# Attention with 32 heads: a small subtraction moves from GpSimd to VectorE, and the sign of its row is turned

## The chip, the cores and the metric

The kernel runs on one core of a Trainium2 chip. The metric is device time in microseconds (us) of one execution. Before the change three runs took 4368.01, 4374.25 and 4378.47 us; their median is 4374.25 us. Engines are named as the profile names them: PE is TensorE (matmul), PEld its weight load, DVE is VectorE, ACT is ScalarE, POOL is GpSimd, SP is SyncE, which here only issues DMAs.

## The reference, cut to what matters

The whole program is eight layers of a network on x of shape (8, 512, 128). The change lies in one of them, an attention with 32 heads of width 32 in each of 8 batch items (worked on in groups of 4 heads: 8 groups in an item, 64 in all):

```python
scale = DIM_HEAD ** (-0.5)
qkv = (x @ w_qkv).reshape(b, n, 3, HEADS, DIM_HEAD)
q, k, v = ...                                  # (b, heads, n, 32)
dots = jnp.einsum('bhnd,bhmd->bhnm', q, k) * scale
attn = jax.nn.softmax(dots, axis=-1)           # exp(dots - max) / sum
out = jnp.einsum('bhnm,bhmd->bhnd', attn, v)
```

## The kernel before, in words

`attend_wide` is the function. It computes the scores twice. The first time (`scores`, L837) queries are rows, and DVE takes each row's maximum from PSUM (`tensor_reduce`, L1046, into `top`). The second time (`shifted_scores`, L843) keys are rows, and the maximum of each query is subtracted inside the matmul: two more rows of the operands carry it, in `q4` the maximum itself and in `k4` a constant, -1.0, set by POOL at L721. ACT then takes the exponential straight from PSUM (L966, into `e`). For precision each number is split in a high part, rounded to fp32r, and a low part, the difference; so there are two rows, one for the high and one for the low part of the maxima.

The way of the maxima, for one group: ACT rounds all 16 columns of `top` into `tops[:, 0]` (`high_tops`, L954); POOL subtracts that from `top` into `tops[:, 1]` (`low_tops`, L726); DVE turns the 128x32 tile (`turn_tops`, L1030, into `topsT`); SP sends it with four small DMAs into the two rows of `q4` (L775); PE needs the rows at the start of the next step.

The work is a pipeline over groups, written out by hand. A step treats group n at stage 0 (projections of q and k; high part by ACT at L939, low part by DVE at L1022; three DMAs of 256 KB for q at L768 and three for k at L781, all on SP's one queue), the group before it at stage 1 (scores and maxima), the one before at stage 2 (the way of the maxima), at stage 3 (shifted scores and exponentials) and at stages 4 and 5 (product with v, sums, normalising). Each engine walks through sixteen places (j, b) of a step, j the head and b the block, and the code says at which place a small operation is put: on DVE the maximum of a place comes first, then what is put there. `low` for q stands at (0, 1), `turn_tops` at (0, 3), `low` for k at (1, 1). On PE `project_k` stands at (0, 3) and `project_v` at (1, 3); `project_v` waits for the low part of k, since they share a PSUM bank. PE starts a step when the six loads of q and k of the group have landed (`loaded`, 16 each) and, for stage 3, when the four row DMAs have (`row_loaded`).

POOL adds pairs of exponential blocks (`e_pair`, L741, four instructions of 128x1024 in a step, with both inputs in SBUF) and multiplies once (`o_norm`, L749). The first of the four waits for PE's sums of the group before (L865, at PE's place (3, 0)). POOL does `low_tops` between the second and the third pair.

Of the kernel before, what the change touches and what calls it, by code (L numbers as in the profile page):

```python
# [20 lines left out]
ALU = mybir.AluOpType  # L21
ACT = mybir.ActivationFunctionType
F32 = mybir.dt.float32
# [9 lines left out]
KROWS = 96  # L33
# [36 lines left out]
def wait(eng, sem, value):  # L70

    if isinstance(value, int) and value <= 0:
        return
    eng.wait_ge(sem, value)
# [572 lines left out]
def attend_wide(nc, g, name, scale):  # L647
# [10 lines left out]
    with Phase(nc, name) as ph:  # L658
# [6 lines left out]
        k4 = [ph.sb(f"k4_{r}", [P, HG, S], F32R) for r in range(RQ)]  # L665
        v4 = [ph.sb(f"v4_{r}", [P, TB, P]) for r in range(2)]
        top = ph.sb("top", [P, 2, HG, TB])
        tops = ph.sb("tops", [P, 2, HG, TB], F32R)
# [11 lines left out]
        set_up, w_loaded = ph.sem("set_up"), ph.sem("w_loaded")  # L680
# [6 lines left out]
        s_ready, max_done, hi_done, lo_done, tops_turned, st_ready, exp_done, pair_done, pv_done, o_copied = (  # L687
            ph.sem(k) for k in ("s_ready", "max_done", "hi_done", "lo_done", "tops_turned", "st_ready", "exp_done",
                                "pair_done", "pv_done", "o_copied"))
# [14 lines left out]
        def next_batch(st):  # L704

            return st.c == U and not (isinstance(st.i, int) and st.i + 1 >= B)

        def run(eng, step):

            for i in range(B):  # L710
                for c in range(1, U + 1):
                    step(Step(i, c, NG, U))
            for c in range(1, 6):
                step(Step(B, c, NG, U))

        with nc.Block() as block:
            @block.gpsimd
            def _(pool):

                for r in range(RQ):  # L720
                    pool.memset(k4[r][KROWS:KROWS + 2].bitcast(F32), -1.0).then_inc(set_up, 1)  # L721

                def low_tops(st):
                    n, t = st.n(2), st.slot(2, 2)
                    pool.wait_ge(hi_done, n)
                    pool.tensor_tensor(tops[:, 1], top[:, t], tops[:, 0].bitcast(F32), ALU.subtract).then_inc(lo_done, 1)  # L726

                def step(st):
                    if st.has(2) and not st.has(4):
                        low_tops(st)  # L730
                    if st.has(4):
                        n, r = st.n(4), st.slot(4, 2)
                        for j in range(HG):
                            if j == 2 and st.has(2):
                                low_tops(st)

                            pool.wait_ge(exp_done, 16 * (n - 1) + 4 * j + 4)
                            if j == 0:

                                wait(pool, sums_done, n - 1)  # L740
                            pool.tensor_tensor(e_pair[:, j, :, :], e[r][:, j, 0:2, :], e[r][:, j, 2:4, :], ALU.add  # L741
                                               ).then_inc(pair_done, 1)
                    if st.has(5):
                        n = st.n(5)
                        pool.wait_ge(o_copied, n)
                        pool.wait_ge(r_done, n)

                        wait(pool, y_ready, n - 1)
                        pool.tensor_tensor(o_norm[:], o_sb[st.slot(5, 2)][:], r_sb[:], ALU.mult).then_inc(o_done, 1)  # L749

                run(pool, step)
# [162 lines left out]
            @block.scalar  # L914
            def _(act):
                def copy_out(st):
                    n = st.n(4)
                    act.wait_ge(pv_done, n)

                    wait(act, o_done, n - 2)  # L920
                    act.activation(o_sb[st.slot(4, 2)][:], g.ps[:, PV_BANK, :], ACT.Copy).then_inc(o_copied, 1)

                def copy_x(batch):
                    act.wait_ge(xp_ready, batch)
                    act.activation(xT[:], g.ps[:, PROJ_BANK, :], ACT.Copy).then_inc(xT_done, 1)

                def copy_x_for_v(st):
                    act.wait_ge(xT_done, st.i + 1)

                    wait(act, v_ready, st.n(4))  # L930
                    act.activation(xT_v[:], xT[:], ACT.Copy).then_inc(xT_v_done, 1)

                def high(st, bank, ready, hi, factor, done):

                    act.wait_ge(ready, st.n(0))
                    if st.has(1):

                        act.wait_ge(loaded[st.slot(1, RQ)], 16 * 6 * st.use(1, RQ))
                    act.activation(hi[:], g.ps[:, bank, :], ACT.Copy, scale=factor).then_inc(done, 1)  # L939

                def copy_v(st):
                    n, r = st.n(3), st.slot(3, 2)
                    act.wait_ge(v_ready, n)

                    wait(act, pv_done, n - 2)
                    act.activation(v4[r][:], g.ps[:, PROJ_BANK, :].rearrange("p (t c) -> p t c", t=TB), ACT.Copy
                                   ).then_inc(v_done, 1)

                def high_tops(st):
                    n, t = st.n(2), st.slot(2, 2)  # L950
                    act.wait_ge(max_done, 16 * n)

                    wait(act, tops_turned, n - 1)
                    act.activation(tops[:, 0], top[:, t], ACT.Copy).then_inc(hi_done, 1)  # L954

                def step(st):
                    for j in range(HG):
                        for b in range(TB):
                            if st.has(3):
                                n, r = st.n(3), st.slot(3, 2)  # L960
                                act.wait_ge(st_ready, 16 * (n - 1) + 4 * j + b + 1)
                                if j == 0 and b == 0:

                                    wait(act, pv_done, n - 2)
                                    wait(act, sums_done, n - 2)
                                act.activation(e[r][:, j, b, :], g.ps[:, ST_BANK + b % 2, :], ACT.Exp  # L966
                                               ).then_inc(exp_done, 1)
                            if (j, b) == (0, 0) and st.has(0):
                                high(st, PROJ_BANK, q_ready, q_hi, scale, q_hi_done)
                            if (j, b) == (0, 1) and st.has(2):  # L970
                                high_tops(st)
                            if (j, b) == (1, 0) and st.has(0):
                                high(st, PROJ_BANK, k_ready, k_hi, 1.0, k_hi_done)
                            if (j, b) == (1, 1) and st.has(3) and st.c == 4:
                                copy_x_for_v(st)
                            if (j, b) == (2, 0) and st.has(3):
                                copy_v(st)
                            if (j, b) == (1, 3) and st.has(4):
                                copy_out(st)
                            if (j, b) == (3, 2) and next_batch(st):  # L980

                                act.wait_ge(k_ready, st.n(0))
                                act.wait_ge(xT_v_done, st.i + 1)
                                copy_x(st.i + 2)

                copy_x(1)
                run(act, step)

            @block.vector
            def _(dve):  # L990
# [7 lines left out]
                def recip(st):  # L998
                    n = st.n(5)
                    dve.wait_ge(l_turned, n)  # L1000
                    dve.reciprocal(r_tok[:], r_sb[:].rearrange("p (c b) -> p c b", b=32)[:, :, 0]
                                   ).then_inc(recip_done, 1)
# [14 lines left out]
                def low(st, bank, hi_done, hi, lo, factor, done):  # L1017

                    dve.wait_ge(hi_done, st.n(0))
                    if st.has(1):  # L1020
                        dve.wait_ge(loaded[st.slot(1, RQ)], 16 * 6 * st.use(1, RQ))
                    dve.scalar_tensor_tensor(lo[:], g.ps[:, bank, :], factor, hi[:].bitcast(F32), ALU.mult,  # L1022
                                             ALU.subtract).then_inc(done, 1)

                def turn_tops(st):
                    n = st.n(2)
                    dve.wait_ge(lo_done, n)
                    if st.has(3):
                        dve.wait_ge(row_loaded[st.slot(3, RQ)], 16 * 4 * st.use(3, RQ))
                    dve.transpose(topsT[:].bitcast(F32), tops[:].rearrange("p h j t -> p (h j t)").bitcast(F32)  # L1030
                                  ).then_inc(tops_turned, 1)
# [4 lines left out]
                def step(st):  # L1036
                    for j in range(HG):
                        for qb in range(TB):
                            if st.has(1):
                                n, t = st.n(1), st.slot(1, 2)  # L1040
# [8 lines left out]
                                low(st, PROJ_BANK, q_hi_done, q_hi, q_lo, scale, q_lo_done)  # L1049
                            if (j, qb) == (0, 1) and st.has(5):  # L1050
                                recip(st)
                            if (j, qb) == (0, 3) and st.has(2):
                                turn_tops(st)
                            if (j, qb) == (1, 0) and st.has(5):
# [1621 lines left out]
```

## Time and profile before

| | |
|---|---|
| runs | 4368.01, 4374.25, 4378.47 us |
| the profiled execution | 4368.01 us, its span 4366.3 us |
| PE busy | 3458.4 us (79%) |
| DVE busy | 3185.1 us (73%) |
| ACT busy | 2437.9 us (56%) |
| POOL busy | 1204.1 us (28%) |
| TensorE's granted clock, mean | 0.902 |
| this attention | about 1290 to 2530 us of the span |

The span is the time from the first to the last instruction of the program; the device time adds 1.7 us. A row of the timeline gives the start, the duration, the engine, the line of the source, what is written and read, and how many instructions of a kind stand in it; in brackets the idle time before it and what ended that. In a row of x2 the duration runs from the start of the first to the end of the second. A weight load or a matmul that waited for a DMA names it.

### The profile page before, as it was taken

How to read it: one execution, taken by the hardware profiler on the slowest of the kernel's cores; microseconds unless marked ns; L12 is line 12 of the kernel's file. 1: busy time of each engine (PE TensorE's matmuls, PEld its weight loads, DVE VectorE, ACT ScalarE, POOL GpSimd, SP SyncE). 2: the span in 40 equal slices, each digit the busy share in tenths (PEclk: the TensorE clock that was granted, in tenths of full speed). 3: DMA queues.
4: the chain of work that ended last, by engine and by line, in shares of the span. 5: the costliest groups of instructions: out<-in, count | busy, mean ns of one | idle time of the engine just before them, and what ended most of it. 6: DMA issues, size and time to landing. Idle time of an engine off the chain costs nothing. (4 is left out here: it accounts for less than half of the span.)

```text
span 4366.3 us, 58109 instructions
## 1 busy us (share of the span) xinstructions
PE 3458.4 (79%) x18272; PEld 2101.5 (48%) x18272; DVE 3185.1 (73%) x7262; ACT 2437.9 (56%) x4422; POOL 1204.1 (28%) x798
## 2 busy tenths in 40 slices
PE   5788888677938999999999937892599998657736
PEld 2555555456714555554555425671366665422214
DVE  3999999566845767767777556684488885789986
ACT  2788888445714656555556514571399997312103
POOL 0000000043413555555555615341000000044520
PEclk9899999888968999999999968896799999877767
DMA  5333332113346766666666401331643432000000
GB/s 183 57 63 64 65 49 34 30 49 122 137 92 79 91 88 90 88 86 88 88 88 88 62 30 50 121 136 55 190 62 43 63 60 41 6 20 5 5 28 25
DMA packets 287698, 307.97 MB, mean 71 GB/s; under 512 B 98031, under 2 KB 187567, under 8 KB 287268
## 3 DMA queue, kind: packets, MB, share of 16 engines
q1 hardware_dynamic: 277668, 283.27, 36.8%
q0 software_dynamic: 9728, 20.99, 1.4%
q8 instruction: 151, 2.47, 0.3%
q14 instruction: 151, 1.24, 0.1%
HBM read 124.40 MB, written 78.05 MB: 46 GB/s over the span
## 5 line engine op out<-in xcount | busy, mean ns | idle before, releaser
L1046 DVE TENSOR_REDUCE at_b_top<-ps 128x1 f32<-128x512 f32 x1024 | 660.9, 682 | 376.5 <-PE ps L837 375.6
L966 ACT ACTIVATE at_b_e<-ps 128x512 f32<-128x512 f32 x1024 | 583.4, 598 | 475.3 <-PE ps L843 461.8
L550 ACT ACTIVATE at_a_e<-at_a_logits,at_a_neg_top 128x512 f32<-128x512 f32 x1024 | 656.2, 716 | 157.0 <-DVE at_a_neg_top L610 155.5
L741 POOL TENSOR_TENSOR at_b_e_pair<-at_b_e 128x1024 f32<-128x1024 f32 x256 | 603.4, 2377 | 479.4 <-PE ps L865 476.9
L474 PE MATMUL ps<-at_a_k,at_a_q 96*128 96x512 f32 x1024 | 477.3, 491 | 185.2 <-DVE at_a_clipped L578 117.3
L837 PE MATMUL ps<-at_b_k,at_b_q 96*128 96x512 f32 x1024 | 501.3, 493 | 40.4 <-DMA at_b_k<-at_b_k_hi 38.1
L543 ACT ACTIVATE at_a_eT<-ps 128x512 f32<-128x512 f32 x896 | 461.3, 588 | 0.7 <-PE ps L487 0.2
L843 PE MATMUL ps<-at_b_q,at_b_k 98*128 98x512 f32 x1024 | 427.5, 419 | 19.1 <-ACT at_b_e L966 18.7
L606 DVE CUSTOM_DVE_ANT_0 at_a_logits<-ps,at_a_strip 128x512 f32<-128x512 f32 x512 | 340.4, 689 | 109.5 <-issue 32.4
L578 DVE TENSOR_SCALAR at_a_clipped<-ps 128x512 f32<-128x512 f32 x512 | 352.0, 688 | 39.8 <-PE ps L474 38.7
L474 PEld LDWEIGHTS ps<-at_a_k,at_a_q 96*128 96x128 f32 x1024 | 185.1, 190 | 397.2 <-DVE at_a_clipped L578 206.4
L600 DVE CUSTOM_DVE_ANT_0 at_a_logits<-at_a_clipped,at_a_decay_strip 128x512 f32<-128x512 f32 x512 | 346.9, 682 | 0.0
L837 PEld LDWEIGHTS ps<-at_b_k,at_b_q 96*128 96x128 f32 x1024 | 197.4, 193 | 274.9 <-issue 110.6
L487 PE MATMUL ps<-ident,at_a_e 128*128 128x128 f32 x2048 | 291.7, 276 | 2.3 <-ACT at_a_eT L543 2.3
L487 PE MATMUL ps<-flip,at_a_e 128*128 128x128 f32 x2048 | 287.8, 273 | 0.2
L1343 POOL TENSOR_TENSOR lin_z<-lin_z,lin_zmax 64x1024 f32<-64x1024 f32 x8 | 31.4, 3926 | 878.1 <-DVE lin_zmax L1440 878.1
L2298 ACT ACTIVATE moe_gate<-ps 128x512 f32<-128x512 f32 x240 | 143.7, 599 | 226.6 <-PE ps L2202 164.4
L487 PEld LDWEIGHTS ps<-ident,at_a_e 128*128 128x128 f32 x2048 | 251.9, 142 | 35.1 <-ACT at_a_e L550 2.5
L843 PEld LDWEIGHTS ps<-at_b_q,at_b_k 98*128 98x128 f32 x1024 | 194.1, 190 | 152.3 <-ACT at_b_e L966 131.0
L487 PEld LDWEIGHTS ps<-flip,at_a_e 128*128 128x128 f32 x2048 | 248.6, 141 | 32.6 <-issue 1.2
L2423 DVE TENSOR_TENSOR moe_h<-moe_gate,ps 128x512 f32<-128x512 f32 x240 | 164.9, 687 | 129.5 <-ACT moe_gate L2298 108.5
L2150 POOL DMA_INDIRECT y_slots<-moe_y_tok,moe_idx x176 | 176.6, 1003 | 282.9 <-DVE moe_y_tok L2411 242.0
(332 smaller groups left out, 6463.3 us busy)
## 6 DMA issues: line engine op xcount, KB each, us to landing
moe_stage<-in_moe_w SPq DMA_DIRECT2D x46, 768.0 KB
at_b_q<-at_b_q_hi SPq DMA_DIRECT2D x128, 256.0 KB, 5.1
at_b_k<-at_b_k_hi SPq DMA_DIRECT2D x128, 256.0 KB, 7.9
v<-in_a_va SPq DMA_DIRECT2D x64, 256.0 KB, 3.7
at_a_v<-v SPq DMA_DIRECT2D x64, 256.0 KB, 7.2
at_b_q<-at_b_q_lo SPq DMA_DIRECT2D x64, 256.0 KB, 7.6
at_b_k<-at_b_k_lo SPq DMA_DIRECT2D x64, 256.0 KB, 8.0
slot_rows<-empty_slots SPq DMA_DIRECT2D x44, 288.0 KB, 6.7
```

The costliest lines, as they stand in the source:

```text
L474: pe.matmul(g.ps[:, S_BANK + qb % 2, :], q4[r][0:KROWS, j, qb * P:(qb + 1) * P], k4[r][0:KROWS, j, :], start=True, stop=True).then_inc(s_r ...
L487: ins = pe.transpose(bank, block, g.ident[:] if decay else g.flip[:])
L543: act.activation(eT[r][:, j, kb, :], g.ps[:, TR_BANK + kb, :], ACT.Copy).then_inc(tr_read[kb], 1)
L550: act.activation(e[:, j, qb, :], logits[:, j % 2, qb, :], ACT.Exp, bias=neg_top[:, j % 2, qb:qb + 1]).then_inc(exp_done, 1)
L578: dve.tensor_scalar(clipped[:, qb, :], g.ps[:, S_BANK + qb % 2, :], -CLAMP, CLAMP, ALU.max, ALU.min).then_inc(clip_done, 1)
L600: dve.tensor_tensor_reduce(logits[:, j % 2, qb, :], clipped[:, qb, :], decay_strip[:, cols], 1.0, -3e38, ALU.mult, ALU.max, top[:, j % 2, ...
L606: dve.tensor_tensor_reduce(logits[:, j % 2, qb, :], g.ps[:, S_BANK + qb % 2, :], strip[:, j, cols], 1.0, -3e38, ALU.add, ALU.max, top[:, j ...
L741: pool.tensor_tensor(e_pair[:, j, :, :], e[r][:, j, 0:2, :], e[r][:, j, 2:4, :], ALU.add).then_inc(pair_done, 1)
L837: pe.matmul(g.ps[:, bank, :], q4[r][0:KROWS, j, qb * P:(qb + 1) * P], k4[r][0:KROWS, j, :], start=True, stop=True).then_inc(s_ready, 1)
L843: pe.matmul(g.ps[:, ST_BANK + kb % 2, :], k4[r][0:KROWS + 2, j, kb * P:(kb + 1) * P], q4[r][0:KROWS + 2, j, :], start=True, stop=True).the ...
L966: act.activation(e[r][:, j, b, :], g.ps[:, ST_BANK + b % 2, :], ACT.Exp).then_inc(exp_done, 1)
L1046: dve.tensor_reduce(top[:, t, j, qb:qb + 1], g.ps[:, bank, :], AX_X, ALU.max).then_inc(max_done, 1)
```

## The change

The subtraction `low_tops` leaves POOL. DVE does it as one `scalar_tensor_tensor`, at place (0, 2), behind the third maximum of the step and ahead of the fourth. ACT now rounds the negated maxima (`scale=-1.0`), DVE computes -top minus the rounded part, and the constant in `k4` becomes +1.0, so the product in the matmul is the same number. The instruction that waits for `hi_done` is now on DVE.

```diff
-                    pool.memset(k4[r][KROWS:KROWS + 2].bitcast(F32), -1.0).then_inc(set_up, 1)
-
-                def low_tops(st):
-                    n, t = st.n(2), st.slot(2, 2)
-                    pool.wait_ge(hi_done, n)
-                    pool.tensor_tensor(tops[:, 1], top[:, t], tops[:, 0].bitcast(F32), ALU.subtract).then_inc(lo_done, 1)
+                    pool.memset(k4[r][KROWS:KROWS + 2].bitcast(F32), 1.0).then_inc(set_up, 1)
 
                 def step(st):
-                    if st.has(2) and not st.has(4):
-                        low_tops(st)
                     if st.has(4):
                         n, r = st.n(4), st.slot(4, 2)
                         for j in range(HG):
-                            if j == 2 and st.has(2):
-                                low_tops(st)
...
-                    act.activation(tops[:, 0], top[:, t], ACT.Copy).then_inc(hi_done, 1)
+                    act.activation(tops[:, 0], top[:, t], ACT.Copy, scale=-1.0).then_inc(hi_done, 1)
...
+                def low_tops(st):
+                    n, t = st.n(2), st.slot(2, 2)
+                    dve.wait_ge(hi_done, n)
+                    dve.scalar_tensor_tensor(tops[:, 1], top[:, t], -1.0, tops[:, 0].bitcast(F32), ALU.mult,
+                                             ALU.subtract).then_inc(lo_done, 1)
...
+                            if (j, qb) == (0, 2) and st.has(2):
+                                low_tops(st)
                             if (j, qb) == (0, 3) and st.has(2):
                                 turn_tops(st)
```

On DVE, in a step of the middle of this attention, this stood before, from the low part of q (L1022) over the second pair of maxima to the low part of k:

```order
L1022 SCALAR_TENSOR_TENSOR at_b_q_lo<-ps,at_b_q_hi 128x512 [waits at_b0_loaded0,at_b0_q_hi_done]
L1001 RECIPROCAL at_b_r_tok<-at_b_r_sb 128x16 [waits at_b0_l_turned]
L1046 TENSOR_REDUCE at_b_top<-ps 128x1 [waits at_b0_s_ready] x2
L1030 STREAM_TRANSPOSE at_b_topsT<-at_b_tops 128x32 [waits at_b0_row_loaded2,at_b0_lo_done]
L1046 TENSOR_REDUCE at_b_top<-ps 128x1 [waits at_b0_s_ready]
L1007 STREAM_TRANSPOSE at_b_r_sb<-at_b_r_tok 128x512 [waits at_b0_recip_done]
```

And this stands there now (the line numbers of the changed file differ by a few):

```order
L1013 SCALAR_TENSOR_TENSOR at_b_q_lo<-ps,at_b_q_hi 128x512 [waits at_b0_loaded0,at_b0_q_hi_done]
L992 RECIPROCAL at_b_r_tok<-at_b_r_sb 128x16 [waits at_b0_l_turned]
L1043 TENSOR_REDUCE at_b_top<-ps 128x1 [waits at_b0_s_ready]
L1019 SCALAR_TENSOR_TENSOR at_b_tops<-at_b_top,at_b_tops 128x16 [waits at_b0_hi_done]
L1043 TENSOR_REDUCE at_b_top<-ps 128x1 [waits at_b0_s_ready]
L1027 STREAM_TRANSPOSE at_b_topsT<-at_b_tops 128x32 [waits at_b0_row_loaded2,at_b0_lo_done]
L1043 TENSOR_REDUCE at_b_top<-ps 128x1 [waits at_b0_s_ready]
L998 STREAM_TRANSPOSE at_b_r_sb<-at_b_r_tok 128x512 [waits at_b0_recip_done]
```

One instruction with the wait for ACT's rounding has come in between two maxima; everything else on DVE keeps its place. On POOL this stood before, for one step:

```order
L741 TENSOR_TENSOR at_b_e_pair<-at_b_e 128x1024 [waits at_b0_sums_done,at_b0_exp_done]
L741 TENSOR_TENSOR at_b_e_pair<-at_b_e 128x1024 [waits at_b0_exp_done]
L726 TENSOR_TENSOR at_b_tops<-at_b_top,at_b_tops 128x16 [waits at_b0_hi_done]
L741 TENSOR_TENSOR at_b_e_pair<-at_b_e 128x1024 [waits at_b0_exp_done] x2
L749 TENSOR_TENSOR at_b_o_norm<-at_b_o_sb,at_b_r_sb 128x512 [waits at_b0_y_ready,at_b0_r_done,at_b0_o_copied]
```

And now, for one step:

```order
L732 TENSOR_TENSOR at_b_e_pair<-at_b_e 128x1024 [waits at_b0_sums_done,at_b0_exp_done]
L732 TENSOR_TENSOR at_b_e_pair<-at_b_e 128x1024 [waits at_b0_exp_done] x3
L740 TENSOR_TENSOR at_b_o_norm<-at_b_o_sb,at_b_r_sb 128x512 [waits at_b0_y_ready,at_b0_r_done,at_b0_o_copied]
```

The four pairs now follow one another with nothing between them that waits for ACT's rounding.

## Rows read from the trace of the kernel before

**Rows 1.** Busy time of each engine over this attention, granted clock, DMA share, GB/s.

```profile
core 0: us, PE busy (x) PEld busy (x) DVE busy (x) ACT busy (x) POOL busy (x), PEclk, DMA share, GB/s
1290.00:2530.00 1240.00, 1180.20 (x6392) 606.52 (x6392) 833.27 (x1438) 708.46 (x1358) 691.13 (x383) 0.98 0.65 84
```

**Rows 2.** Waits of the weight loads, 1400 to 2480 us: total, times, longest.

```profile
PEld ps L837 <- DMA at_b_k<-at_b_k_hi: 25.9, 57, 1.0
```

**Rows 3.** Timeline of PE at two starts of a step (third row: the later start).

```profile
1898.46 0.50 PE L837 MATMUL ps<-at_b_k,at_b_q 96*128 96x512 f32 x1 [0.17 <-DMA at_b_k<-at_b_k_hi]
...
1916.38 0.50 PE L843 MATMUL ps<-at_b_q,at_b_k 98*128 98x512 f32 x1
1916.77 0.50 PE L837 MATMUL ps<-at_b_k,at_b_q 96*128 96x512 f32 x1
```

**Rows 4.** Timeline of SP's queue in the step from 1898.46 to 1916.77.

```profile
1901.64 1.20 SPq L768 DMA_DIRECT2D at_b_q<-at_b_q_hi  x2
...
1904.27 2.64 SPq L775 DMA_DIRECT2D at_b_q<-at_b_topsT  x4
1907.15 0.59 SPq L781 DMA_DIRECT2D at_b_k<-at_b_k_hi  x1
```

**Rows 5.** The DMA engines within that step, columns as in the first group.

```profile
1902.50:1914.50 12.00, 11.76 (x72) 6.65 (x71) 8.36 (x14) 7.50 (x14) 5.00 (x3) 1.00 1.02 130
```

**Rows 6.** Timelines of SP and PE in the fourth and the sixth step.

```profile
1340.88 1.19 SPq L768 DMA_DIRECT2D at_b_q<-at_b_q_hi  x2
...
1345.47 0.59 SPq L781 DMA_DIRECT2D at_b_k<-at_b_k_hi  x1
...
1356.29 0.79 PE L837 MATMUL ps<-at_b_k,at_b_q 96*128 96x512 f32 x1 [5.44 <-DMA at_b_k<-at_b_k_hi]
...
1380.73 1.19 SPq L768 DMA_DIRECT2D at_b_q<-at_b_q_hi  x2
...
1386.76 0.59 SPq L781 DMA_DIRECT2D at_b_k<-at_b_k_hi  x1
...
1396.33 0.39 PE L837 MATMUL ps<-at_b_k,at_b_q 96*128 96x512 f32 x1
```

**Rows 7.** Timeline of DVE around the change, step from 1898.46.

```profile
1902.83 1.29 DVE L1046 TENSOR_REDUCE at_b_top<-ps 128x1 f32<-128x512 f32 x2 [1.06 <-PE ps L837]
1904.04 0.20 DVE L1030 STREAM_TRANSPOSE at_b_topsT<-at_b_tops 128x32 f32<-128x32 f32 x1
1904.64 0.69 DVE L1046 TENSOR_REDUCE at_b_top<-ps 128x1 f32<-128x512 f32 x1 [0.40 <-PE ps L837]
...
1906.45 0.67 DVE L1022 SCALAR_TENSOR_TENSOR at_b_k_lo<-ps,at_b_k_hi 128x512 fp32r<-128x512 f32 x1
```

**Rows 8.** Timeline of POOL in the same step.

```profile
1896.62 4.71 POOL L741 TENSOR_TENSOR at_b_e_pair<-at_b_e 128x1024 f32<-128x1024 f32 x2 [7.72 <-PE ps L865]
1901.35 0.22 POOL L726 TENSOR_TENSOR at_b_tops<-at_b_top,at_b_tops 128x16 fp32r<-128x16 f32 x1
1901.53 4.73 POOL L741 TENSOR_TENSOR at_b_e_pair<-at_b_e 128x1024 f32<-128x1024 f32 x2
```

**Rows 9.** A small instruction of the same kind on DVE: busy us, mean ns.

```profile
L138 DVE SCALAR_TENSOR_TENSOR st_ffn_t<-st_ffn_t,st_ffn_var 128x32 f32<-128x32 f32 x6 | 1.2, 192 | 0.2
```

**Rows 10.** Linear attention: timelines of POOL and DVE, then one line's ns min/median/max.

```profile
3936.52 2.33 POOL L1343 TENSOR_TENSOR lin_z<-lin_z,lin_zmax 64x1024 f32<-64x1024 f32 x1 [22.13 <-DVE lin_zmax L1440]
...
3937.68 1.73 DVE L1450 TENSOR_TENSOR lin_yT<-lin_y 128x512 f32<-128x512 f32 x1
...
L1450 DVE TENSOR_TENSOR lin_yT<-lin_y x8: 693/1734/1735, 3892.3 to 4202.4; 128x512 f32<-128x512 f32 x8
```

**Rows 11.** Linear attention: POOL's products beside DVE's scans, ns min/median/max.

```profile
L1361 POOL TENSOR_TENSOR lin_prod<-lin_state,lin_phi x56: 1254/2172/2181, 3866.2 to 4185.9; 128x512 f32<-128x512 f32 x56
```

**Rows 12.** Timelines of POOL and DVE in the step after the longest one.

```profile
1840.00 4.70 POOL L741 TENSOR_TENSOR at_b_e_pair<-at_b_e 128x1024 f32<-128x1024 f32 x2 [7.54 <-PE ps L865]
...
1846.74 1.29 DVE L1046 TENSOR_REDUCE at_b_top<-ps 128x1 f32<-128x512 f32 x2 [1.08 <-PE ps L837]
```

**Rows 13.** Timeline of PE: the projection of v, step from 1898.46.

```profile
1908.13 1.06 PE L829 MATMUL ps<-at_b_w,at_b_xT_v 128*128 128x128 f32 x8
```

## The prediction, made before the changed kernel ran

> **What bounds the kernel now.** I read the busy time by stretch first. The change lies in the 1240 us from 1290 to 2530, with 64 groups, so about as many steps. PE is busy 1180 of them, DVE 833, POOL 691 [rows 1]. That looks like a stage bound by PE, and the second view corrects it. Of the 59 steps between 1400 and 2480 us, 57 begin with a weight load that waited for the last load of k [rows 2]. The timeline of PE shows it in place: the first matmul at 1898.46 waited for that DMA, and at the next start, 1916.77, 0.39 us lie between two matmuls that otherwise stand closer [rows 3]. So a step ends when the third load of k lands, and its length is a loop: PE projects q, ACT and DVE split it, SP issues q's loads 3.18 us after the start (1901.64), then the rows of maxima (1904.27), then k's loads (1907.15) [rows 4]; the DMA engines are full without a gap from 1902.5 to 1914.5 [rows 5], and k lands just ahead of 1916.77. From 1396.33 to 1898.46 there are 27 steps [rows 3, 6]: 502.13 / 27 = 18.60 us each. PE alone needs less: the step from 1898.46 took 18.31, with 0.15 or so of waiting in it, so 18.15 to 18.3.
>
> What matters is then not how busy DVE or POOL is, but whether the change makes (a) q's loads start later, (b) k's loads land later, or (c) PE itself take over 18.6 us in a step.
>
> **What it removes.** POOL loses 64 subtractions of 0.22 us (14 us). POOL waited 7.72 us in the step for PE's sums [rows 8] and has that slack every step, so this is worth nothing. Its effect is on phase: the third and fourth pair now start 0.22 us earlier or more. The turn on DVE did not wait for POOL: the subtraction ended at 1901.57, the turn began at 1904.04 behind the fourth maximum [rows 7, 8]. So no wait is removed either. The factor -1.0 on ACT and the +1.0 in two rows are the same instructions with other constants: 0.
>
> **What it adds.** 64 small instructions on DVE. The nearest row is the same operation on 32 columns, 192 ns [rows 9]; following instructions start about 80 ns before the one ahead ends, so 0.11 us each in a row. It waits for ACT's rounding, which had ended by 1901.35, when POOL began to use it [rows 8], while DVE gets there at 1903.44 (the fourth maximum's start: 1902.83 plus the 0.61 by which two maxima are apart) [rows 7]. So the added wait is over 2 us early. Queued behind it are the fourth maximum, the turn, the fifth maximum and k's low part. DVE idles 0.40 us ahead of the fifth [rows 7], so the plain cost, 0.11 and at most 0.22 us, ends there. Only the rows' DMAs go out 0.1 to 0.2 us later, and k's loads behind them at most as much.
>
> Does a later issue of k's loads matter? In the fourth step they went out 4.59 us after q's, and the next step began 15.41 us after q's (1340.88, 1345.47, 1356.29). In the sixth they went out 6.03 us after, and the next began 15.60 after [rows 6]. The step at 1898.46 has 5.51 and 15.13 [rows 3, 4]. Issue 1.44 us later, landing at most 0.19 us later: the loads queue behind q's in full DMA engines anyway. So up to half a microsecond there costs nothing. By this sum alone the change is worth 0.
>
> **The term that can cost.** The added instruction reads `top` and `tops[:, 0]`, both in SBUF, while POOL runs its pairs, which read SBUF too. Nothing on DVE in this stage did so. In the linear attention something does: `lin_yT<-lin_y`, two inputs in SBUF, took 1.73 us in seven of its eight executions and 0.693 in the one without POOL. In the shown case it began at 3937.68, POOL's instruction ended at 3938.85, it ended at 3939.41: 0.56 after POOL's end, though it needs 0.69 [rows 10]. So it stood still until 0.14 us before POOL's recorded end and then ran. The products of POOL beside DVE's scans go from 1254 to 2172 ns in the same manner, by turns, one instruction of each [rows 11].
>
> The Trainium skill has this as a rule (SBUF — State Buffer, "Who interferes with whom"): a VectorE instruction with two SBUF inputs and a GpSimd instruction that reads SBUF exclude each other for the whole instruction, and the one that comes second fully blocks. By that rule, the trace agrees, at 1.73 against 0.69 us.
>
> So what counts is where DVE's 1903.44 falls among POOL's pairs. POOL's pairs start 2.33 us apart. Without the subtraction the fourth starts 7.0 us after the first: 1896.62 + 7.0 = 1903.62 [rows 8]. DVE asks at 1903.44, 0.18 us before the third pair gives way. It waits 0.1 to 0.2 us, harmless by the slack above. But had it asked just after 1903.62, it would wait for the fourth pair: 2.38 - 0.14 = 2.24 us. I worked this distance out in the same way for 59 steps (from the first pair's start and the fourth maximum's; first 0.59 us, last 0.15): mean 0.2, on time in 53, late in 6, and under 0.1 us on time in 7 more. The late ones follow the longest steps: after the one of 19.1 us the fourth pair starts at 1840.00 + 7.0 = 1847.00 and DVE asks at 1846.74 + 0.61 = 1847.35 [rows 12].
>
> Price of a late step: the fourth maximum starts 2.24 + 0.11 later, at 1905.79; the turn 1906.40; the fifth 1906.52 instead of 1904.64, so 1.88 later, and so is the end of k's low part (1907.12, now 1909.00) [rows 7]. PE's projection of v, at 1908.13, waits for that low part [rows 13]: PE stands 0.9 us. PE's step becomes 18.15 + 0.9 to 18.3 + 0.9, against 18.60: 0.45 to 0.6 us more. k's loads go out behind the rows at 1906.6 + 2.64 = 1909.25, 7.6 us after q's; the trace shows up to 6.03 hidden. Beyond that, between 0 and 1.6 us. I take 0.5 for a late step, since the DMA engines still have q's data then, and keep 0.45 to 1.6. A late step also protects the next: it has no wait for landing, and that wait is what makes DVE late against POOL.
>
> **Sum.** 6 late steps, 8 with a few of the near ones, times 0.5 = 4 us; the rest 0. The profiled execution took 4368.01, so 4372. That execution lies 6.2 below the median of the runs, 4374.25; by the median the forecast is 4378. About 0.2% (9 us) is what a measurement of this kernel can tell from no change.
>
> **Rivals.**
> - The edge lies elsewhere (slower). The start and the lock need not coincide to 0.1 us. If the decision falls 0.15 to 0.2 us against DVE, over half the steps are late; since a late step makes the next on time, some 24 of 59 are. At 0.5 to 0.8 us that is 12 to 19 us: 4390. For it: the mean distance is as small as the uncertainty. Against: in the linear attention both engines' turns are clean.
> - POOL, with its next pair queued, gets in ahead of DVE each time. Then DVE waits out the fourth pair in all 59 steps, with 0.2 to 0.5 us on top: k's low part 2.3 us late, PE stands 1.3 to 1.45, the step 19.5 to 19.6, 1.0 more: +59, 4433. Against: the alternation [rows 11].
> - The small instruction is not held up, because it is so short. Then nothing is left of the cost: 4374.
> - Faster: taking POOL out of the chain from maxima to rows lets something start earlier. The only place is the start and end of the stage, where a few waits of under 2 us could go; 4372. Over 9 us would need the DMA loop to shorten by 0.15 us in each step, and its start (q's low part) is ahead of the change.
>
> **Chances.** Forecast 0.56; edge elsewhere 0.24; POOL ahead each time 0.06; not held up 0.10; faster path 0.04. Slower by over 0.2%: most of the second case, the third, and a small part of the first, 0.30. Faster by over 0.2%: 0.05, with the scatter of the loop. Within: 0.65. The range 4367 to 4395 takes in the scatter of the runs before below, and 24 late steps at 0.8 us above; it leaves out the third case and a late step of 1.6 us.
>
> **What would show it.** DVE's new instruction takes from 0.2 to 0.7 us where POOL's third pair is about to end, and 2.3 to 2.5 us in a late step; a count of the two gives the number. In late steps PE's projection of v waits for k's low part. Elsewhere steps still start on k's landing, 18.6 us apart, with k's loads issued up to 0.4 us later. If the instruction always takes 0.2 us, the lock is not there for it; if it takes over 2 us in most steps, the forecast is wrong; and if k lands later in steps where it took 0.5, the claim that the issue is hidden is wrong.

## The result, and the profile after

The changed kernel takes 4400.49 us (median of five runs, 4398.01 to 4405.13), the kernel before 4371.31 (five runs, 4367.10 to 4378.47). The ratio is 1.0056, 95% interval 1.0041 to 1.0070: slower by 0.41 to 0.70%. On record beside it are 22 runs of the changed kernel, the five among them (4382.46 to 4406.04, median 4397.12); it fits these, while the two medians above alone would give 1.0067. The forecast was 4378 with a range to 4395. In the profiled executions the span went from 4366.3 to 4388.6 us, 22.3 us more, and all of it lies in this attention, which now ends about 23 us later:

```profile
core 0: us, PE busy (x) PEld busy (x) DVE busy (x) ACT busy (x) POOL busy (x), PEclk, DMA share, GB/s
1290.00:2553.00 1263.00, 1184.01 (x6392) 604.15 (x6392) 907.45 (x1502) 707.27 (x1358) 679.33 (x319) 0.98 0.62 82
```

Against [rows 1] PE's busy time is the same within 4 us, the granted clock too. DVE shows 74 us more for 64 added instructions, over 1 us each, where a like one took 0.19 [rows 9]: they stand and wait. The distribution for that one line, in ns min/median/max:

```profile
L1019 DVE SCALAR_TENSOR_TENSOR at_b_tops<-at_b_top,at_b_tops x64: 165/660/3633, 1321.9 to 2515.2; 128x16 fp32r<-128x16 f32 x64
```

Now the waits, 1400 to 2500 us (total us, times, longest). The first row is of PE and new; the second, of the weight loads, answers to [rows 2], where the number was 57 (in a window 20 us shorter):

```profile
PE ps L820 <- DVE at_b_k_lo L1013: 20.5, 24, 1.1
...
PEld ps L828 <- DMA at_b_k<-at_b_k_hi: 15.7, 36, 1.0
```

In 24 steps PE's projection of v stood for k's low part. I took the 58 steps from the sixth on one by one (start of the first matmul to the next start). In 25 the added instruction takes over 2 us; I call these late. They last 19.48 us on average, the other 33 last 18.54. Before the change the same 58 steps last 18.57 on average (the 18.60 of the prediction is from 27 of them). So the late ones add 25 x 0.91 = 22.7 us and the others save 1.1: together 21.6 of the 22.3 us.

One such step, and the step after it, in the timelines of POOL and DVE:

```profile
1791.28 9.41 POOL L732 TENSOR_TENSOR at_b_e_pair<-at_b_e 128x1024 f32<-128x1024 f32 x4 [7.03 <-PE ps L856]
...
1811.07 9.39 POOL L732 TENSOR_TENSOR at_b_e_pair<-at_b_e 128x1024 f32<-128x1024 f32 x4 [7.03 <-PE ps L856]
```

```profile
1797.69 3.04 DVE L1019 SCALAR_TENSOR_TENSOR at_b_tops<-at_b_top,at_b_tops 128x16 fp32r<-128x16 f32 x1
1800.65 0.68 DVE L1043 TENSOR_REDUCE at_b_top<-ps 128x1 f32<-128x512 f32 x1
...
1803.15 0.67 DVE L1013 SCALAR_TENSOR_TENSOR at_b_k_lo<-ps,at_b_k_hi 128x512 fp32r<-128x512 f32 x1
...
1817.50 0.66 DVE L1019 SCALAR_TENSOR_TENSOR at_b_tops<-at_b_top,at_b_tops 128x16 fp32r<-128x16 f32 x1
```

The pairs are 2.34 us apart, so the fourth starts at 1798.30 and at 1818.09. DVE asks (the recorded start of its instruction) at 1797.69 and at 1817.50: 0.61 and 0.59 us ahead of the fourth pair. The second time it gets in when the third pair ends. The first time it is there just as early and POOL's fourth pair goes first; DVE ends at 1800.73, with the fourth pair (1791.28 + 9.41 = 1800.69). PE, at the projection of v, and the two starts around the step:

```profile
1792.80 0.39 PE L828 MATMUL ps<-at_b_k,at_b_q 96*128 96x512 f32 x1
...
1803.91 1.13 PE L820 MATMUL ps<-at_b_w,at_b_xT_v 128*128 128x128 f32 x8 [1.09 <-issue]
...
1812.58 0.41 PE L828 MATMUL ps<-at_b_k,at_b_q 96*128 96x512 f32 x1
```

PE stands 1.09 us ahead of the projection, which begins as k's low part ends (1803.15 + 0.67); the trace names no releaser in this one case of the 25. The step takes 19.78 us; the next, by its start at 1830.80, 18.22. Of the 25 late instructions, 4 asked after the fourth pair had begun, 12 asked 0.06 to 0.18 us ahead of it, and 9 asked 0.31 to 0.61 us ahead and still lost. Of the 33 others, 6 asked 0.11 to 0.20 us ahead and 27 over 0.3 us ahead.

### The profile page after: what moved, and what is told of

Read it like the earlier page. It is cut to its first block and busy times, and to the rows that moved or that the text cites. A ratio compares the mean times of both kernels' runs of the same rounds, so it can differ in the third digit from the quotient of the medians.

```text
span 4388.6 us, 58109 instructions
## 1 busy us (share of the span) xinstructions
PE 3462.0 (79%) x18272; PEld 2099.5 (48%) x18272; DVE 3259.7 (74%) x7326; ACT 2437.3 (56%) x4422; POOL 1191.8 (27%) x734
```

## The experiments

Theory: a VectorE instruction with two inputs in SBUF and a GpSimd instruction that reads SBUF exclude each other, and the late steps are all of the cost. Each kernel has 4 to 11 runs, compared with 12 or 21 of the kernel before on the same chip: medians 4367.8 us for e1 to e4, 4369.2 for e5 to e8, 4367.1 for e9 to e11. Steps are counted in the one profiled execution of each.

**e1, the move alone.** The signs as before.

```diff
-  dve.scalar_tensor_tensor(tops[:, 1], top[:, t], -1.0, tops[:, 0].bitcast(F32), ALU.mult, ALU.subtract)
+  dve.tensor_tensor(tops[:, 1], top[:, t], tops[:, 0].bitcast(F32), ALU.subtract)
-  act.activation(tops[:, 0], top[:, t], ACT.Copy, scale=-1.0)          # and the rows 1.0
+  act.activation(tops[:, 0], top[:, t], ACT.Copy)                      # and the rows -1.0
```

> The subtraction moved to VectorE alone, as a tensor_tensor, with the signs as before the change (factor 1 on ScalarE, -1.0 in the two rows). Theory (VectorE and GpSimd exclude each other while both read SBUF): as the changed kernel, 20 to 30 of 58 steps with the small instruction over 2 us long, 20 to 35 us slower than before. Rival (the sign, another operation, or the scale on ScalarE costs): within 5 us of before.

Measured: 4394.80 us, ratio 1.0059 (1.0046 to 1.0073), 29 late steps (a thirtieth instruction took 1.99 us). The sign, the scale and the kind of instruction show no effect; the move is all.

**e2, POOL out of the way; e10, only ahead of the fourth pair.**

```diff
   for j in range(HG):
+      if j == 2 and st.has(2):          # e10: j == 3
+          pool.wait_ge(lo_done, st.n(2))
       pool.wait_ge(exp_done, ...)
```

> The changed kernel, but GpSimd waits for the small instruction of VectorE before its third pair, so that it is idle when VectorE asks. Theory (exclusion): the small instruction takes 0.2 us in all 64 cases, no late step, the time of before within 5 us; GpSimd's third and fourth pair end 2 us later, at about 9.9 us of the step, which nobody awaits before 14.6. Rival (the instruction and its wait in VectorE's row cost by themselves): stays 20 to 35 us slower than before. Rival (GpSimd's pairs are near the path): slower than the changed kernel.

> The changed kernel, but GpSimd waits for VectorE's small instruction before its fourth pair (not its third). VectorE still meets the third pair and waits up to its end. Theory (what costs is only the fourth pair getting in ahead): the small instruction takes 0.2 to 0.7 us, never over 1; no late step; within 5 us of before. Rival (meeting a pair at all costs): 10 us or more slower than before.

Measured: e2 4369.26 us, 1.0001 (0.9992 to 1.0010); e10 4370.19 us, 1.0007 (0.9997 to 1.0016). No late step in either. The same instruction with the same wait at the same place of DVE, in e2:

```profile
L1021 DVE SCALAR_TENSOR_TENSOR at_b_tops<-at_b_top,at_b_tops x64: 162/166/1116, 1325.5 to 2494.9; 128x16 fp32r<-128x16 f32 x64
```

So the instruction in DVE's row costs nothing; neither does meeting the third pair, in e10 (median 242 ns, against 166 here). The one of 1.1 us here and those of 1.3 and 1.1 in e10 lie behind the 58 steps. Only the fourth pair costs.

**e3, one operand in SBUF.** The low part of the maxima is left out: its row stays zero.

```diff
-  dve.scalar_tensor_tensor(tops[:, 1], top[:, t], -1.0, tops[:, 0].bitcast(F32), ALU.mult, ALU.subtract)
+  dve.tensor_reduce(scr[:], <tops[:, 0] as 128x16x1>, AX_X, ALU.max)
```

> The changed kernel with a small instruction of VectorE at the same place, behind the same wait, that reads one 128x16 operand from SBUF instead of two and writes a spare tile; the low part of the maxima is left out (its row stays zero). Theory (two inputs in SBUF are what excludes): the small instruction takes about 0.17 us always, no late step, the time of before within 5 us. Rival (any instruction there costs, or any reading beside GpSimd): 20 to 35 us slower than before, small instruction still up to 2.7 us.

Measured: 4367.30 us, 0.9995 (0.9986 to 1.0004).

```profile
L1020 DVE TENSOR_REDUCE at_b_scr<-at_b_tops x64: 157/159/170, 1324.9 to 2494.5; 128x16 f32<-128x16 f32 x64
```

At most 170 ns in 64 cases, beside the same pairs. This changed the kind of instruction along with the number of inputs. That the kind is not the reason can be read in the changed kernel: q's low part is the same operation as the added one, runs beside the pairs too (POOL's second), and has one input in PSUM and one in SBUF. It was never held up:

```profile
L1013 DVE SCALAR_TENSOR_TENSOR at_b_q_lo<-ps,at_b_q_hi x64: 674/681/692, 1282.7 to 2478.9; 128x512 fp32r<-128x512 f32 x64
```

So a second input in SBUF is what makes it wait.

**e4, asking earlier.** The instruction at (0, 1), where DVE idles 1.1 us afterwards.

```diff
-  if (j, qb) == (0, 2) and st.has(2):
+  if (j, qb) == (0, 1) and st.has(2):
       low_tops(st)
```

> The changed kernel with the small instruction at place (0, 1), behind the reciprocal. VectorE asks about 3.2 us after the step's start, at or just after the start of GpSimd's third pair (2.8 to 3.2), so it waits 1.9 to 2.4 us nearly always, 1.1 of which it idled before. If it gets in at every pair's end: k's low part 0.5 us later, ahead of the projection of v, no late step, within 5 us of before although the instruction takes 2 us. If GpSimd's queued next pair gets in ahead in a share of the cases (9 of some 40 in the changed kernel): that share has a wait of 4.3 us and a step of over 20 us; 12 such steps make 20 us or more over before.

Measured: 4419.45 us, 1.0114 (1.0099 to 1.0130). In 14 of the 58 steps DVE asked at the very end of the second pair, by the records 0.01 us ahead of the third, and always got in, in 0.11 us. In the other 44 it met the third. In 25 of these it got in at that pair's end, after 1.6 to 2.3 us, and the steps last 18.61 us on average, as the same 25 did before (18.60): 2 us of wait, nothing lost. But 19 of the 44 times POOL's fourth pair went ahead and DVE stood over 4 us:

```profile
1762.30 9.37 POOL L732 TENSOR_TENSOR at_b_e_pair<-at_b_e 128x1024 f32<-128x1024 f32 x4 [7.43 <-PE ps L856]
```

```profile
1767.23 4.48 DVE L1019 SCALAR_TENSOR_TENSOR at_b_tops<-at_b_top,at_b_tops 128x16 fp32r<-128x16 f32 x1
```

DVE was there 2.1 us ahead of the fourth pair (1762.30 + 7.02) and ended at 1771.71 with it. Coming early doesn't help.

The 19 steps fall in two groups. Eight last 20.35 us on average. The other eleven last 22.10, this one among them, since TensorE's granted clock fell in them as well. PE had waited for a maximum behind DVE's long instruction; then the clock was 0.50, the lower of its two levels (1.2 of 2.4 GHz):

```profile
1772.37 0.50 PE L828 MATMUL ps<-at_b_k,at_b_q 96*128 96x512 f32 x1 [1.99 <-DVE at_b_top L1043]
```

```profile
1774.00:1776.00 2.00, 2.00 (x12) 0.21 (x4) 1.39 (x3) 0.00 (x0) 1.27 (x1) 0.50 0.04 6
```

The sixteen products with v behind that wait took 3.25 us instead of 1.92. In the other eight the clock stayed at 1.00, though PE had waited 1.5 to 2.1 us in them and 1.7 to 2.1 in the eleven; what decides is open. In the kernel before and in the changed one the clock fell in none of the 58 steps, so it has no part in the 22 us.

**e5, the reading alone.** The kernel before, with a spare instruction.

```diff
+  if (j, qb) == (0, 2) and st.has(2):
+      dve.wait_ge(hi_done, st.n(2))
+      dve.scalar_tensor_tensor(scr[:], top[:, st.slot(2, 2)], -1.0, tops[:, 0].bitcast(F32), ALU.mult, ALU.subtract)
```

> The kernel before, GpSimd keeping its subtraction, with one more instruction on VectorE at place (0, 2): the same two inputs in SBUF, written to a spare tile nobody reads. Theory (exclusion): GpSimd's fourth pair starts about 0.22 us later here than in the changed kernel, so VectorE always asks ahead of it; no step is late by missing the edge, and late steps come only where GpSimd's queued fourth pair gets in ahead of the waiting VectorE, 20 to 45% of the steps as in the runs so far: 12 to 26 late steps of about 0.9 us, 10 to 24 us slower than before. If only the missed edge counted: within 5 us of before.

Measured: 4388.77 us, 1.0041 (1.0029 to 1.0054). All 58 asked 0.41 to 0.79 us ahead of the fourth pair; 12 lost to it, with steps of 19.94 us on average. The missed edge is thus not needed for a loss.

**e6, one wait in every step.** The instruction at (0, 3).

```diff
-  if (j, qb) == (0, 2) and st.has(2):
+  if (j, qb) == (0, 3) and st.has(2):
       low_tops(st)
```

> The changed kernel with the small instruction at place (0, 3), behind the fourth maximum. VectorE asks at 5.6 us of the step, after GpSimd's fourth pair has begun (5.1 to 5.5) and waits to that pair's end (7.4 to 7.8) in nearly every step; behind that pair stands o_norm, which waits for VectorE, so nothing gets in ahead. Theory: 50 or more of 58 instructions take 1.7 to 2.2 us, k's low part ends at about 10.3 us, the projection of v 0.6 us late, each step 0.3 to 0.5 longer, evenly: 17 to 29 us slower than before. Rival (a late step costs by the irregularity, not by PE's wait): under 10 us.

Measured: 4413.29 us, 1.0101 (1.0086 to 1.0115): 44 us where 17 to 29 were expected. The instruction waits for the end of the fourth pair in all 58 steps, as expected; a step takes 19.30 us. PE's projection of v starts at 10.35 to 10.64 us of the step (mean 10.53), against 9.68: 0.85 late where I had expected 0.6. Behind it 8.7 to 8.9 us follow, against 8.89 on average before, so little of the delay is made good. I had taken PE's own step for 18.15 to 18.3; by 9.68 + 8.70 it is nearer 18.35.

**e7, shorter pieces.** Each pair cut in two.

```diff
-  pool.tensor_tensor(e_pair[:, j, :, :], e[r][:, j, 0:2, :], e[r][:, j, 2:4, :], ALU.add).then_inc(pair_done, 1)
+  for h in range(2):
+      ins = pool.tensor_tensor(e_pair[:, j, h, :], e[r][:, j, h, :], e[r][:, j, 2 + h, :], ALU.add)
+  ins.then_inc(pair_done, 1)
```

> The changed kernel with each of GpSimd's four pairs cut in two instructions of 128x512 (eight of about 1.2 us instead of four of 2.37). VectorE still meets GpSimd every time. Theory: a wait that goes to the end of one more instruction costs 1.2 us instead of 2.35, so k's low part is at most 1.0 us late and ends by about 9.7, when PE comes to the projection of v; few steps or none are longer: within 8 us of before, though the small instruction takes up to 1.6 us. Rival (any collision costs a step 0.9 us): 20 us or more slower than before.

Measured: 4480.76 us, 1.0258 (1.0245 to 1.0272), far off what I expected. POOL and DVE in one step:

```profile
1900.12 9.94 POOL L733 TENSOR_TENSOR at_b_e_pair<-at_b_e 128x512 f32<-128x512 f32 x8 [7.03 <-PE ps L858]
```

```profile
1907.22 2.87 DVE L1021 SCALAR_TENSOR_TENSOR at_b_tops<-at_b_top,at_b_tops 128x16 fp32r<-128x16 f32 x1
```

DVE asks in the sixth piece and ends at 1910.09, with the eighth (1910.06). Of the 59 times that it asked in the sixth piece, it got in at that piece's end 12 times and stood through two more pieces to the end of the queue 47 times; at the end of the seventh it never got in. So a late instruction waited longer than before (2.9 to 3.6 us), the 46 late ones of the 58 steps last 20.43 us on average, and in six of them the granted clock fell as in e4. A shorter piece is no shorter wait, if the next one goes ahead. (The profiled execution, 4460.53 us, is the fastest of the six.)

**e9, a gap.** A small memset on POOL, which reads nothing, between the third and fourth pair.

```diff
   for j in range(HG):
+      if j == 3:
+          pool.memset(scr[:], 0.0)
       pool.wait_ge(exp_done, ...)
```

> The changed kernel with a small memset of a spare 128x16 tile on GpSimd between its third and fourth pair. It reads nothing from SBUF, so between the reading of the two pairs there is a gap. Theory that VectorE loses at a pair's end only because the next reading instruction follows without a gap: no instruction that asks over 0.3 us ahead of the fourth pair loses any more; left are the misses of the edge, 4 to 10 late steps of 0.9 to 1.1 us: 3 to 11 us slower than before. Rival (the loss comes from something else, as GpSimd's turn in a queue): 20 to 29 late steps and 20 to 30 us as in the changed kernel.

Measured: 4373.01 us, 1.0012 (1.0003 to 1.0021). All 53 that asked over 0.14 us ahead of the fourth pair got in; the 5 others, from 0.30 us behind its start to 0.05 ahead, are the 5 late steps (19.18 us), 3 us together; the interval of the ratio, 1 to 9 us, takes that in. A step near the edge, POOL and DVE:

```profile
1802.49 7.05 POOL L735 TENSOR_TENSOR at_b_e_pair<-at_b_e 128x1024 f32<-128x1024 f32 x3 [7.84 <-PE ps L859]
1809.49 0.11 POOL L729 MEMSET at_b_scr<- 128x16 f32 x1
1809.55 2.38 POOL L735 TENSOR_TENSOR at_b_e_pair<-at_b_e 128x1024 f32<-128x1024 f32 x1
```

```profile
1809.37 0.21 DVE L1022 SCALAR_TENSOR_TENSOR at_b_tops<-at_b_top,at_b_tops 128x16 fp32r<-128x16 f32 x1
```

DVE asks 0.18 us ahead of the fourth pair and is through in 0.21. In the changed kernel 12 of 18 that asked 0.06 to 0.2 us ahead lost; here all 25 that asked 0.14 to 0.21 us ahead got in.

**e11, PE not waiting.** The projection of v later on PE, its copy later on ACT.

```diff
-  if (j, b) == (1, 3) and st.has(3):   project_v(st)      # ACT: copy_v at (2, 0)
+  if (j, b) == (2, 1) and st.has(3):   project_v(st)      # ACT: copy_v at (2, 2)
```

> The changed kernel with PE's projection of v at place (2, 1) instead of (1, 3), and its copy by ScalarE at (2, 2) instead of (2, 0), so that a late low part of k meets no waiting PE. 20 to 30 late instructions as in the changed kernel. If PE's wait for k's low part is the price of a late step, and the later landing of k beside it a smaller one (k lands 0.6 to 0.7 us later in late steps of the changed kernel): a late step costs 0.6 to 0.7 instead of 0.9, 14 to 20 us slower than before. If PE's wait were all: within 8 us of before. If k's landing were all: no change, 25 to 30 us. A part of the steps may change by 0.1 to 0.2 us because the projections of v and of the output now stand close together on PE.

Measured: 4394.42 us, 1.0063 (1.0050 to 1.0077): 27 us where 14 to 20 were expected. PE no longer waits for k's low part. A late step takes 19.04 us instead of 19.48, less than expected, but 50 of 58 are late (waits from 1.9 us counted) where 20 to 30 were expected, 46 of them by asking after the fourth pair's start. PE now stands at the step's start, for k's landing (waits 1400 to 2500 us):

```profile
PE ps L828 <- DMA at_b_k<-at_b_k_hi: 22.7, 55, 0.9
```

That wait lies between POOL's first pair and DVE's asking, so a late landing makes the next step late: 41 of 49 late steps were followed by another. PE also waits for maxima of DVE there (20.9 us in 51 places), which it hardly did before.

**e8, the loop itself.** The kernel before, with one place changed.

```diff
-  if (j, qb) == (0, 1) and st.has(0):
+  if (j, qb) == (0, 0) and st.has(0):
       low(st, PROJ_BANK, q_hi_done, q_hi, q_lo, scale, q_lo_done)
```

> The kernel before with VectorE's low part of q at place (0, 0) instead of (0, 1), ahead of the second maximum; nothing else. Theory that a step's length is set by the loop from q's low part over the DMA queue to k's landing: q's loads go out 0.2 us earlier and each step is 0.2 us shorter until PE's own 18.2 to 18.3 us: 8 to 15 us faster than before. Rival (PE or the maxima set the step): the same as before or slower, since the second maximum is 0.4 us later.

Measured: 4357.01 us, 0.9971 (0.9960 to 0.9982), faster than both kernels. q's loads go out 2.97 us after the start instead of 3.18, a step takes 18.39 us instead of 18.57: 58 x 0.18 = 10 us. The weight loads' waits for the landing (1400 to 2480 us), against [rows 2]:

```profile
PEld ps L837 <- DMA at_b_k<-at_b_k_hi: 13.5, 40, 0.6
```

## Why the prediction was wrong, point by point

- **What bounds a step** was right: k's landing, in a loop from q's low part. e8 starts q's loads 0.21 us earlier and shortens the step by 0.18.
- **Nothing removed, plain cost nothing** was right: e2 and e3 show the instruction, its wait and its place at 1.0001 and 0.9995.
- **The term that can cost** was right in kind: two inputs in SBUF beside POOL's pairs, harmless up to the third pair's end, costly with the fourth. e3, e5 and e10 show each half.
- **The count** is the step that failed. "It waits 0.1 to 0.2 us, harmless", for any asking ahead of the fourth pair, gave 6 to 8 late steps; there were 25. From the turns in the linear attention [rows 11] I concluded that DVE gets in at the end of the instruction it waits for. It does not surely: among those over 0.3 us ahead, 9 of 36 lost here, 17 of 37 in e1, 12 of 58 in e5 (all over 0.4 us), and nearer to the fourth pair's start 12 of 18. The start itself was missed 4 times, where 6 were forecast. The rival in which POOL gets in ahead had the right mechanism and was priced for every step, at 59, with 0.06; the rival of the edge had the right number, 24, by luck: its cause does not fit the 9 cases of over 0.3 us, nor 8 of the 12 nearer ones, which asked 0.14 us or more ahead, where with a gap (e9) all got in. What happened is that POOL gets in ahead in a share of the cases, and neither rival said that.
- **The price** of a late step was put at 0.5 us and is 0.91. k's low part came 2.0 us late on average (10.68 against 8.67 us of the step) where 1.88 was forecast, and up to 2.4 where DVE had waited 0.6 us and lost. PE's projection of v began 1.06 us late, against 0.9, and only 0.15 us of that was made good at the next start, against 0.3 to 0.45: PE's own length is about 18.35, not 18.15 to 18.3. k itself landed at 19.31 us of a late step instead of 18.52, 0.79 us later, so the landing alone would have cost nearly as much. 8 x 0.5 = 4 against 25 x 0.91 = 23.
- **"A late step protects the next"**: half true. Behind a late step DVE asked at least 0.31 us ahead in every case, so the start of the fourth pair was never missed. But only 17 of the 25 next steps were on time; in 8 POOL went ahead all the same. e11 shows where the protection came from: without PE's wait, it turns into its opposite.
- **k's later issue is hidden**: true for the 0.6 us by which k's loads went out later where DVE waited 2 us and got in (e4, k landing at 18.55 us of the step against 18.52). With 2.2 us of later issue (e6) k lands at 19.10, so 0.6 us later.
- The runs' median moved by 29 us (26 with the 22 runs), the profiled executions by 22. e1, the same move, had 29 late steps in its profiled execution and 35 us. That the number of late steps varies from run to run is an argument, not shown: the other runs have no trace.

## What to carry to other kernels

Before a small instruction moves to VectorE, look at how many of its inputs lie in SBUF and what GpSimd reads at that moment; a second SBUF input beside a row of GpSimd instructions can cost not the rest of the one under way but the next ones too. If it must stand there, give GpSimd a wait or a gap at that point: the wait ahead of the fourth pair brought the time back to that of the kernel before (e10, 1.0007). And a stage whose PE looks 95% busy can be bound by a DMA that lands at each step's start: one operation moved by one place in that loop gave 12 us (e8).

## What the runs showed of the hardware that was not expected

- A VectorE instruction that waits for GpSimd does not always come next. Behind 128x1024 additions in a row it lost 19 of 44 (e4) to 12 of 58 (e5) times, though it had asked 0.4 to 2.2 us ahead; behind 128x512 additions it stood to the queue's end in 47 of 59 (e7). With a memset of 0.11 us in between it never lost when over 0.14 us ahead (e9, 53 of 53). In the linear attention of the same program the two engines took turns [rows 11]: from 3950 us on they end at 3950.12 (DVE), 3951.17 (POOL), 3952.26, 3953.31 and so forth. What decides a single case stays open: in the changed kernel, of ten that asked 0.58 to 0.59 us ahead nine got in, of six at 0.60 to 0.61 two.
- The Trainium skill (SBUF — State Buffer, "Who interferes with whom") has two SBUF inputs as the condition; e3 agrees, with at most 0.17 us where there is one. Its rule (same page, "Summary: rules for kernel authors") that the second to issue blocks until the first finishes agrees where DVE asked after the fourth pair's start: 2.0 to 2.3 us in those 4 cases for an instruction of 0.17. For the 21 late ones that asked ahead of it, "until the first finishes" was too short: they stood to the end of the pair behind, 2.5 to 3.0 us.
